# Five instead of three buffers for the high and low parts of q and k, in an AdaLN block with two attentions

## The reference, cut to what matters

```
mod = (silu(c) @ wmod).reshape(4, 6, 1, 256)             # sa, ca, ga, sb, cb, gb
h = layernorm(x) * (1 + ca) + sa
x = x + ga * favor_attention(h)                          # 16 heads of 16, 64 random features a head
h = layernorm(x) * (1 + cb) + sb
x = x + gb * ffn(h)

def ffn(x):                                              # 4 experts = 4 chunks of 512 tokens
    for e in range(4):
        xn = layernorm(x[:, chunk e]) * norm_w + norm_b
        xm = xn[..., :256 >> e]                          # chunk 0: 256 columns, 1: 128, 2: 64, 3: 32
        q, k, v of chunk e = xm @ (q_w, k_w, v_w)[:, :m].T + biases
    attn = softmax(q @ k.T / 16)                         # 8 heads of 32, 2048 keys, exact
    out of chunk e = (attn @ v)[..., :m] @ o_w[:m, :m].T + o_b[:m] + x
```

## Time and profile before

| what | value |
|---|---|
| time, median of 3 runs | 1766.48 us (1762.68 to 1766.83) |
| profiled execution, its own time | 1768.27 us |
| its span, first to last instruction | 1766.5 us |
| TensorE matmul, busy | 1678.5 us, 95% |
| VectorE, busy | 1385.5 us, 78% |
| GpSimd, busy | 1126.5 us, 64% |
| ScalarE, busy | 1085.4 us, 61% |
| mean granted TensorE clock | 0.974 of full speed |

### The profile page before, as it was taken

One profiled execution on the slowest core, in us unless ns is written; L12 is line 12 of the kernel. 1 busy time (PEld: TensorE's weight loads), 2 busy tenths in 40 slices (PEclk: granted clock), 3 DMA queues, 4 the chain that ended last, 5 costly groups with the idle time before them and its releaser, 6 DMA issues.

```text
span 1766.5 us, 32009 instructions
## 1 busy us (share of the span) xinstructions
PE 1678.5 (95%) x11538; PEld 970.8 (55%) x11538; DVE 1385.5 (78%) x2629; ACT 1085.4 (61%) x2066; POOL 1126.5 (64%) x1058
## 2 busy tenths in 40 slices
PE   6999989999999989999999998999999999899998
PEld 4776544444577554444467755444437765444443
DVE  5987978787688788787678878877858878787783
ACT  1885536566688553565668844466667875356665
POOL 2784358767678344867767734686686862477675
PEclk8999989999999998999999999999999999899999
DMA  6000360010200045001110005400120001520101
GB/s 188 2 1 1 103 188 15 19 46 25 73 2 1 1 152 143 10 19 46 58 40 2 2 16 174 106 19 10 46 72 25 2 1 58 179 61 18 39 17 48
DMA packets 56077, 89.57 MB, mean 51 GB/s; under 512 B 13288, under 2 KB 31976, under 8 KB 53100
## 3 DMA queue, kind: packets, MB, share of 16 engines
q1 hardware_dynamic: 54768, 87.45, 17.0%
q10 hardware_dynamic: 1152, 0.07, 0.0%
HBM read 49.29 MB, written 35.72 MB: 48 GB/s over the span
## 4 chain that ended last, share of the span: by engine, by line
PE 68%; DVE 16%; ACT 9%; DMA 2%; issue 2%; SPq 1%; POOL 1%; ACTq 0%; DVEq 0%; POOLq 0%
PE PS L1530 13%; PE PS L1705 12%; PE PS L1717 12%; PE PS L1730 6%; PE PS L1424 5%; DVE MXP L1111 4%; PE PS L1449 4%; PE PS L1432 3%; PE PS L1459 3%; ACT HT L670 2%; ACT HTR L673 2%; DVE STAT L1004 2%; ACT PR L901 2%; DVE QKS L1179 1%; ACT PHIQ L711 1%
## 5 line engine op out<-in xcount | busy, mean ns | idle before, releaser
L631 POOL TENSOR_TENSOR TS<-PR 128x1024 f32<-128x1024 f32 (+1 forms) x248 | 551.6, 2238 | 259.8 <-ACT PR L901 195.4
L1111 DVE TENSOR_REDUCE MXP<-PS 128x1 f32<-128x512 f32 x960 | 589.0, 681 | 145.9 <-PE PS L1530 145.2
L901 ACT ACTIVATE PR<-PS 128x512 f32<-128x512 f32 x960 | 487.6, 622 | 285.3 <-PE PS L1705 261.8
L1530 PE MATMUL PS<-KOP,QOP 96*128 96x512 f32 x960 | 406.8, 437 | 10.2 <-DVE MXP L1111 3.5
L1705 PE MATMUL PS<-QOP,KOP 97*128 97x512 f32 x960 | 376.5, 424 | 3.5 <-ACT QOP L888 3.1
L1530 PEld LDWEIGHTS PS<-KOP,QOP 96*128 96x128 f32 x960 | 186.2, 195 | 169.3 <-issue 90.4
L1705 PEld LDWEIGHTS PS<-QOP,KOP 97*128 97x128 f32 x960 | 180.3, 190 | 143.7 <-ACT PR L901 110.2
L1717 PE MATMUL PS<-PR,V 128*32 128x512 f32 x1920 | 255.1, 597 | 0.5
L1730 PE MATMUL PS<-TS,ones 128*32 128x512 f32 x960 | 136.0, 604 | 6.7 <-DVE TS L1289 6.7
L1717 PEld LDWEIGHTS PS<-PR,V 128*32 128x32 f32 x1920 | 62.2, 110 | 140.6 <-issue 98.4
L549 POOL TENSOR_SCALAR PK<-XSK 128x1024 f32<-128x1024 f32 x64 | 67.2, 1050 | 100.3 <-ACT XSK L733 100.3
(11 more groups left out here) (157 smaller groups left out, 2524.1 us busy)
## 6 DMA issues: line engine op xcount, KB each, us to landing
KOP<-k_scr SPq DMA_DIRECT2D x84, 256.0 KB, 5.7
k_scr<-QKS SPq DMA_DIRECT2D x64, 256.0 KB, 2.9
QOP<-q_scr SPq DMA_DIRECT2D x180, 64.0 KB, 2.0
q_scr<-QKS SPq DMA_DIRECT2D x40, 256.0 KB, 3.0
X<-in_L_attn_x_dram SPq DMA_DIRECT2D x16, 512.0 KB, 3.9
out_dram<-X SPq DMA_DIRECT2D x12, 512.0 KB, 3.0
QOP<-MXT SPq DMA_DIRECT2D x224, 0.5 KB
KOP<-QKS SPq DMA_DIRECT2D x36, 64.0 KB, 2.0
```

The costliest lines, as they stand in the source:

```text
L631: g.tensor_tensor(sums(k)[:, 0:len(stage)], pair[:, :, 0], pair[:, :, 1], ALU.add).then_inc(S["psum_t"], 1)
L901: a.activation(PR[:, k % 2, w, q], bank(score_bank(p, n, w, q)), ACT.Exp).then_inc(S["ex"], 1)
L1111: v.tensor_reduce(MXP[:, u % 2, i, kc:kc + 1], bank(max_bank(p)), AX.X, ALU.max).then_inc(S["am_rd"], 1)
L1530: mm(bank(max_bank(p)), QOP[0:96, u % QS6, i * P:(i + 1) * P], KOP[0:96, h % KS6, kc * CH:(kc + 1) * CH], start=True, stop=True).then_inc( ...
```

## The change

`QKS` gets five buffers instead of three (`QKB = 5`), and the two added ones are the tiles of `XSQ`, which now is a view of buffers 3 and 4. Every `n % 3` and `n - 3` becomes `n % QKB` and `n - QKB`. With it come three more edits:

- `load_queries`: SyncE loads a slot's queries after the stores of the next slot, and waits there only for the stores of query blocks.
- The eps and the negated mean go from VectorE (`statistics`) to GpSimd (`deviations`, `deviations_again`).
- `VECTOR_SUMS` gets step 62: VectorE makes the last three pair sums of a batch.

```diff
+    QKB = 5
-    QSN = [len(range(i, NQ, 3)) for i in range(3)]
+    QSN = [len(range(i, NQ, QKB)) for i in range(QKB)]
-        QKS = sb("QKS", [P, 3, 2, CH], F32R)
-        XSQ = sb("XSQ", [P, 2, NH * NM])
+        QKS = sb("QKS", [P, QKB, 2, CH], F32R)
+        XSQ = QKS[:, QKB - 2:].bitcast(F32).rearrange("p a h n -> p a (h n)")
-        VECTOR_SUMS = (SLOTS - 3, SLOTS - 1)
+        VECTOR_SUMS = (SLOTS - 3, SLOTS - 2, SLOTS - 1)
-            return scr[n % 3], 32 * (QSN[n % 3] * b + n // 3 + 1)
+            return scr[n % QKB], 32 * (QSN[n % QKB] * b + n // QKB + 1)
+                def load_queries(s):
+                    wait_all(sp, *[stored(b, n) for n, t in blocks(s) if t >= 2])
+                    for u in range(QS6):
+                        if units[u][1] == expert[s]:
+                            load_q(b, u)
...
-                    n0 = blocks(s)[0][0]
-                    wait_all(sp, stored(b, n0), stored(b, n0 + 2))
+                    if s > 0:
+                        load_queries(s - 1)
                     if s == 0:
+                        sp.wait_ge(*stored(b, 0))
                         sp.wait_ge(S["num"], 2 * NC * (b + 1))
...
-                    for u in range(QS6):
-                        if units[u][1] == e:
-                            load_q(b, u)
+                load_queries(NC - 1)
...
                 def deviations_again(s, h):
                     cols, n = halves(s, h), 2 * (NC * b + s) + h + 1
                     wait_all(pool, (S["ve3"], 2 * n))
+                    g.tensor_scalar(VE[:, cols], MV[:, cols, 1], NORM_EPS, None, ALU.add).then_inc(S["ve3_e"], 1)
+                    g.tensor_scalar(NEGM[:, cols], MV[:, cols, 0], -1.0, None, ALU.mult).then_inc(S["negm"], 1)
+                    wait_all(pool, (S["ve3_e"], n))
                     g.tensor_tensor(RSTD[:, cols], VE[:, cols], minus_half[:, cols], ALU.pow).then_inc(S["rs3"], 1)
...
-                        pool.wait_ge(*stored(b, NQ - 2))
+                        wait_all(pool, *[stored(b, n) for n in range(NQ - QKB, NQ) if n % QKB >= 2])
...
-                    if n >= 3:
-                        act.wait_ge(*stored(b, n - 3))
+                    if n >= QKB:
+                        act.wait_ge(*stored(b, n - QKB))
...
-                        wait_all(act, stored(b, NQ - 3), stored(b, NQ - 1))
+                        wait_all(act, *[stored(b, n) for n in range(NQ - QKB, NQ) if n % QKB < 2])
...
-            def statistics(tiles, srcs, signal, negated=False):
+            def statistics(tiles, srcs, signal):
...
                 for t in tiles:
-                    v.bn_aggr(MV[:, t], STAT[:, t]).then_inc(S["dve_own"], 1)
-                    own.n += 1
-                dve.wait_ge(S["dve_own"], own.base + own.n)
-                sl = slice(tiles[0], tiles[-1] + 1)
-                if negated:
-                    v.tensor_scalar(NEGM[:, sl], MV[:, sl, 0], -1.0, None, ALU.mult).then_inc(S[signal], 1)
-                v.tensor_scalar(VE[:, sl], MV[:, sl, 1], NORM_EPS, None, ALU.add).then_inc(S[signal], 1)
+                    v.bn_aggr(MV[:, t], STAT[:, t]).then_inc(S[signal], 1)
...
+                        pair_sum(b, SLOTS - 2)
                         pair_sum(b, SLOTS - 1)
```

More of the change, by code:

```diff
@@ L221, in adaln_block @@
                    den den_sb num num_sb denT rec rb rT mt yps x1
-                   ve2 rs3 rstd2 ve3 nmr3 h2 x2 x2T xn_sb qp q_hi q_lo scr0 scr1 scr2 vp v2_sb vb_ok obm
+                   ve2 ve2_e rs3 rstd2 ve3 ve3_e negm nmr3 h2 x2 x2T xn_sb qp q_hi q_lo scr0 scr1 scr2 scr3 scr4 vp v2_sb vb_ok obm
                    q_in0 q_in1 q_in2 q_in3 q_in4 q_in5 kf0 kf1 kf2 kf3 k_in1 k_in2 k_in3 k_in4 k_in5 k_in6 k_in7
@@ L232, in adaln_block @@
         ov = out.rearrange("b (c t p) d -> p (b c) t d", p=P, t=TPC)
-        scr = [S[f"scr{i}"] for i in range(3)]
+        scr = [S[f"scr{i}"] for i in range(QKB)]
         st = [S[f"st{i}"] for i in range(NC)]
@@ L404, in batch @@
                                 sp.dma_start(KOP[r:r + DH, 0, e * CH:(e + 1) * CH].bitcast(F32),
-                                             QKS[0:DH, n % 3, half].bitcast(F32)).then_inc(S[f"kf{e}"], 16)
+                                             QKS[0:DH, n % QKB, half].bitcast(F32)).then_inc(S[f"kf{e}"], 16)
                         for half in range(2):
                             sp.dma_start(dst[half, j * P:(j + 1) * P, e * CH:(e + 1) * CH],
-                                         QKS[:, n % 3, half].bitcast(F32)).then_inc(scr[n % 3], 16)
+                                         QKS[:, n % QKB, half].bitcast(F32)).then_inc(scr[n % QKB], 16)
                         if s == NC - 1 and t == 0:
@@ L570, in deviations @@
                     cols, n = halves(s, h), 2 * (NC * b + s) + h + 1
-                    wait_all(pool, (S["ve2"], n))
+                    wait_all(pool, (S["ve2"], 2 * n))
+                    g.tensor_scalar(VE[:, cols], MV[:, cols, 1], NORM_EPS, None, ALU.add).then_inc(S["ve2_e"], 1)
+                    wait_all(pool, (S["ve2_e"], n))
                     g.tensor_tensor(RSTD[:, cols], VE[:, cols], minus_half[:, cols], ALU.pow).then_inc(S["rstd2"], 1)
@@ L576, in deviations_again @@
                     wait_all(pool, (S["ve3"], 2 * n))
+                    g.tensor_scalar(VE[:, cols], MV[:, cols, 1], NORM_EPS, None, ALU.add).then_inc(S["ve3_e"], 1)
+                    g.tensor_scalar(NEGM[:, cols], MV[:, cols, 0], -1.0, None, ALU.mult).then_inc(S["negm"], 1)
+                    wait_all(pool, (S["ve3_e"], n))
                     g.tensor_tensor(RSTD[:, cols], VE[:, cols], minus_half[:, cols], ALU.pow).then_inc(S["rs3"], 1)
-                    wait_all(pool, (S["rs3"], n))
+                    wait_all(pool, (S["rs3"], n), (S["negm"], n))
                     g.tensor_tensor(NMR[:, cols], NEGM[:, cols], RSTD[:, cols], ALU.mult).then_inc(S["nmr3"], 1)
@@ L804, in high_part @@
                     act.wait_ge(S["qp"], NQ * b + n + 1)
-                    if n >= 3:
-                        act.wait_ge(*stored(b, n - 3))
+                    if n >= QKB:
+                        act.wait_ge(*stored(b, n - QKB))
                     for s2 in range(1, NC):
-                        if blocks(s2)[0][0] == n - 3:
+                        if blocks(s2)[0][0] == n - QKB:
                             act.wait_ge(S[f"kf{expert[s2]}"], 48 * (b + 1))
-                    a.activation(QKS[:, n % 3, 0], bank(ring(("q", s, n))), ACT.Identity, bias=qk_bias(t)
+                    a.activation(QKS[:, n % QKB, 0], bank(ring(("q", s, n))), ACT.Identity, bias=qk_bias(t)
                                  ).then_inc(S["q_hi"], 1)
@@ L1173, in statistics_of_h @@
                     dve.wait_ge(S["h2"], TPC * (NC * b + s) + 2 * h + 2)
-                    statistics(halves(s, h), [Hh[:, t] for t in halves(s, h)], "ve3", negated=True)
+                    statistics(halves(s, h), [Hh[:, t] for t in halves(s, h)], "ve3")
                 def low_part(s, i):
@@ L1178, in low_part @@
                     dve.wait_ge(S["q_hi"], NQ * b + n + 1)
-                    v.scalar_tensor_tensor(QKS[:, n % 3, 1], bank(ring(("q", s, n))), qk_bias(t),
-                                           QKS[:, n % 3, 0].bitcast(F32), ALU.add, ALU.subtract
+                    v.scalar_tensor_tensor(QKS[:, n % QKB, 1], bank(ring(("q", s, n))), qk_bias(t),
+                                           QKS[:, n % QKB, 0].bitcast(F32), ALU.add, ALU.subtract
                                            ).then_inc(S["q_lo"], 1)
```

## The result

| | before | after |
|---|---|---|
| time, median of 8 runs each | 1766.82 us (1762.68 to 1770.24) | 1776.70 us (1773.18 to 1782.04) |
| after / before | | 1.0061, 95% interval 1.0046 to 1.0075 |
| span of the profiled execution | 1766.5 us | 1778.0 us |
| TensorE busy / VectorE busy | 1678.5 / 1385.5 us | 1673.0 / 1373.2 us |
| mean granted TensorE clock | 0.974 | 0.969 |

A forecast was written before the change was run, and what follows sets the result against it. TensorE was taken as the bound, with 68% of the chain of waits. 4 x 2.0 - 3 x 1.1 = +4.7 us on 1768.27 gave 1773.0; the median being 1.8 lower, the forecast was 1771, range 1758 to 1782.

The forecast's parts named there:

- Loss at unit 0's loads: Before each batch's first maxima: TensorE waits for queries now loaded behind block 5's stores; 5.8 us lost first, idle 7 us.
- the clock stretch behind it: Behind unit 0's wait: 3.03 us of TensorE work takes 5.4 us at halved clock, block 6 starting 8.2 us late.
- Rival 1: Late loads cost more: landing near 3.8 us, clock low for 6 us; +3.9 us a batch, 1780 us; chance 0.22.
- stage bound of 3.9 us: Upper bound of the middle stage's loss per batch: loads land in 3.8 us and the clock costs 3.0.
- Rival 4: Unit 0's wait hidden, old store wait gone: block 10's keys about 5.1 us earlier, 1743 us; chance 0.06.
- The nine loads moved: Between block 9's stores and block 10's keys: issue takes 4.03 us, ending at 665.4, just when the low part is there.
- behind it the order is the same: After the maxima of block 10's keys: the sum ends there, 1.7 to 2.0 us late, nothing added up to the first score.
- Third pair sum: At a batch's end: VectorE also sums step 62, so step 63 ends earlier; 1.1 us gained, three times.
- my upper case: Third pair sum if XH does not hold VectorE up: step 63's sum ends 1.45 us earlier.
- The lower case: Third pair sum if GpSimd's XH holds VectorE up: 0.7 us gained, by the skill's rule of shared SBUF interfaces.
- Statistics: Eps and negated mean to GpSimd: VectorE loses 3.8 us a batch, priced at nothing beyond 0.5 us ahead of block 5.

The follow-up runs named there:

- Experiment 8: The changed kernel with slot 1's nine query loads put behind the keys and stores of block 10, unit 0's loads left late; 1766.21 us.
- experiment 9: Experiment 8 with the first three maxima made behind block 8 instead of block 5 on TensorE and VectorE; 1734.57 us.
- experiment 3: The changed kernel with unit 0's loads behind slot 0's stores and the nine loads behind block 10's keys and stores; 1728.95 us.
- experiment 11: Experiment 3 with block 12 (TensorE) and the low parts of blocks 11 and 12 (VectorE) ahead of the maxima of block 10's keys; 1735.63 us.
- experiment 2: The changed kernel with only unit 0's three loads put back behind the stores of slot 0; 1742.83 us.
- experiment 1: The changed kernel with each slot's query loads behind that slot's own stores again, as in the kernel before; 1749.63 us.
- experiment 4: Experiment 1 without the empty wait, SyncE's wait for the stores of blocks 8 and 9 in slot 2, which has no queries to load; 1734.76 us.
- experiment 7: The kernel before with only the two small edits, statistics to GpSimd and the third pair sum on VectorE; 1751.99 us.
- experiment 10: Experiment 3 with three buffers instead of five and the feature scores in a tile of their own; 1738.46 us.

## Why the prediction was half right

1. *Loss at unit 0's loads: right.* The wait was forecast at 7.0 us and is 7.50; the clock stretch behind it (maxima to block 6) at 5.4 and is 5.13. Rival 1's reasons for a larger loss (a landing of 3.8 us, a clock low for 6 us) didn't come, though its number, 1780, is nearer than mine; its own stage bound of 3.9 us was passed for the reasons in 2 and 3. Rival 4, which had this wait hidden, fell, as argued: its loads can't come before block 5. Experiment 8 prices the late loads of unit 0 at 37.3 us, 9.3 a batch, and experiment 9 shows that it is the standing still.
2. *"The nine loads moved": this step failed.* Up to block 10's low part the sum holds: forecast 18.7 us after the first maxima, measured 18.6. Then I took 4.03 us for the nine loads from a row where the queue was empty, because SyncE had just waited for its stores to land. Moved straight behind eight stores they take 5.67, and the keys of block 10, forecast 0.3 us behind their low part, are issued 2.3 us behind it. In the second batch, from which I forecast, F to K is 24.14 us where I had 22.4, and this explains it. Over the four batches F to K got shorter by 3.0 us a batch, not 4.0. What in the queue holds the issue up stays open; experiment 3 shows that the place of the loads decides.
3. *The clock after that wait: missing.* My sum ended at the keys' maxima and had "behind it the order is the same". The order is, the clock isn't: +1.2 us a batch up to the first score. The experiments bear it out in the main (without 11, which changes this stretch): where the wait before the keys' maxima was 1.9 us or less, K to S is 5.3 to 5.9 us, but once 6.3; where it was over 2 us, it is 6.2 to 7.6 in 14 of 17 batches. In the other three (waits of 2.5, 2.8 and 3.3 us) it is 5.3 to 5.5, and in experiment 11 the clock fell behind waits of 0.6 to 0.9 us. So the length of the wait alone doesn't decide, and what does stays open.
4. *Third pair sum: right in kind, 1.1 forecast, 3.0 measured.* I left out the clock here as well, though the slow group at 463.32 stood in the trace, and the sum itself gained a little more than my upper case. The lower case, that XH holds VectorE up, was wrong: VectorE isn't held up. I had read it from a rule that the two contend, and that doesn't say who waits.
5. *Statistics: 0.5 us a batch, 2.0 in all, and nothing beyond; measured 4.7 in all.* TensorE's 0.67 us of idle in 47 was mostly a wait for VectorE (0.51), and taking it away gave 0.93 up to W, more than all the idle time that the window showed. Beside it the stage to the first score got shorter, which I had priced at nothing.
6. *Rival 4's number, 1743, came out in experiment 2 (1742.8), for other reasons.* The stage gained 2.9 us a batch there and not 5.1, and the small edits 15.0 us and not 3.3. Its own case, five buffers with the loads left where they were, is experiment 1, and there the stage gained 1.8 us a batch. The 5.1 came only in experiment 4: I had overlooked the empty wait, which stands ahead of block 10's keys before as well. Loads and waits set right give 13.5 us with three buffers (experiment 7 to 10), and five buffers 9.5 us on top (experiment 10 to 3). How much of the 13.5 is the empty wait alone no run shows; with five buffers it was 14.9.
7. S to E is 0.4 to 1.0 us longer in each batch after. It varies between 205.6 and 207.9 us over all these kernels without a pattern that I can name; it stays open.

Errors 2 and 3 made the loss larger, 4 and 5 made the gain larger; they half cancel, and the net was off by 5 us only. That 1776.7 lies within my range is therefore in good part luck: both terms of the sum lie outside their own bounds.

## What to carry to other kernels

When a load is moved behind stores, price its issue by a row where stores stand ahead of it and not by a row from an empty queue, and look for waits in the issuing queue that guard nothing. When a wait of TensorE comes or goes, read the granted clock behind it and add or take off the slow stretch, at each place, also small ones; here it followed most waits over 2 us. More buffers paid here only with the loads that share their queue standing where nobody waits for them, so try the place of the loads, and the waits beside them, first.

## What I had not expected of the hardware

- Issuing a 64 KB load took SyncE 0.42 us on a quiet queue and up to 1.52 us (1.81 in the whole run) within 4 us of eight 256 KB stores, around which the DMA share was 1.06: issue time is not a constant of the instruction.
- VectorE's sum of two 128x1024 tiles took 1.23 us when GpSimd's TENSOR_SCALAR began during it, and that one grew from 1.23 to 2.04; when it began during GpSimd's two-tile sum it took 2.96, and that one was not stretched (2.36).
- TensorE's work behind a wait of 2.03 us ran at 1.2 GHz, behind three of 0.63 to 0.77 us too (experiment 11), and behind 3.29 us once at full speed (experiment 2, first batch):

```profile
228.93 0.96 PE L1537 MATMUL PS<-KOP,QOP 96*128 96x512 f32 x3 [3.29 <-DMA KOP<-QKS]
```
